# Rotary embedding of the queries: the cosine product stays in the PSUM bank, and the bank is freed one step later

## The reference, cut to what matters

```python
x = layernorm(x + gelu(einsum("bds,st->bdt", x, (w1 @ w2.T) * sparse_mask) + b2))  # applied per position of width 512
x = layernorm(x + cross_attention(x, ctx, ctx, mask, wq, wk, wv, wo))   # 32 query heads, 8 key heads
x = layernorm(x + x @ W.T + b + routed LoRA)
```

```python
x1, x2 = x[..., :64], x[..., 64:]
return concatenate([x1 * cos - x2 * sin, x2 * cos + x1 * sin], axis=-1)
```

## Time and profile before

| What | us |
|---|---|
| median of the three runs shown | 557.63 |
| the three runs | 554.43, 557.63, 2854.0 |
| the profiled execution: span from first to last instruction | 555.4 |
| TensorE busy | 510.5 (92%) |
| VectorE busy | 464.5 (84%) |
| ScalarE busy | 285.9 (51%) |
| GpSimd busy | 274.5 (49%) |
| one iteration of the loop (six alike, from 118 to 441.4) | 53.9 |

### The profile page before, as it was taken

The page is one execution under the profiler, slowest core; times in us unless marked ns, Lnnn a source line. Parts: engine busy times, 40 slices in busy tenths (PEclk is TensorE's granted clock), DMA queues, the critical chain, the costliest instruction groups (busy, mean ns, idle before and its releaser), DMA issues.

```text
span 555.4 us, 8155 instructions
## 1 busy us (share of the span) xinstructions
PE 510.5 (92%) x2637; PEld 419.9 (76%) x2637; DVE 464.5 (84%) x766; ACT 285.9 (51%) x494; POOL 274.5 (49%) x327
## 2 busy tenths in 40 slices
PE   5999788998999899989999999999899999979993
PEld 3776667886888687878877887788688788757882
DVE  3567877988899899989998899799979978989667
ACT  4373247763475347625761775267526642644423
POOL 2046445467256625652575267427723762316824
PEclk9999899999999999999999999999999999989998
DMA  8910220030103100320022011202020200300004
GB/s 301 342 39 1 73 80 1 1 113 6 71 2 113 40 36 0 113 75 0 23 90 76 0 56 57 76 0 96 17 76 0 76 1 8 52 1 0 2 1 151
DMA packets 27452, 31.45 MB, mean 57 GB/s; under 512 B 6177, under 2 KB 14625, under 8 KB 27434
## 3 DMA queue, kind: packets, MB, share of 16 engines
q1 hardware_dynamic: 27434, 31.22, 17.2%
HBM read 29.12 MB, written 2.10 MB: 56 GB/s over the span
## 4 chain that ended last, share of the span: by engine, by line
PE 54%; DVE 23%; issue 11%; ACT 5%; POOL 3%; DMA 2%; DVEq 0%; SPq 0%; ACTq 0%; POOLq 0%
PE bank L212 16%; PE bank L214 15%; PE bank L213 15%; PE bank L284 5%; DVE QR L951 5%; DVE VWl L850 3%; ACT QS L577 3%; PE bank L222 2%; DVE MX L968 2%; DVE PTl L850 2%; DVE QA L940 1%; ACT VWh L577 1%; DVE KR L935 1%; DMA WQr<-in_L_xattn_wq_dram 1%; DVE X L907 1%
## 5 line engine op out<-in xcount | busy, mean ns | idle before, releaser
L1393 POOL TENSOR_TENSOR PB<-SM,RI 128x512 f32<-128x512 f32 x32 | 34.1, 1067 | 149.1 <-DVE RI L981 149.1
L577 ACT ACTIVATE VWh<-bank 64x512 fp32r<-64x512 f32 x128 | 75.7, 591 | 61.1 <-PE bank L214 59.9
L577 ACT ACTIVATE QS<-bank 64x512 f32<-64x512 f32 x128 | 75.8, 592 | 59.1 <-DVE QR L951 49.3
L212 PE MATMUL bank<-XTh,WQh 128*128 128x512 f32 x256 | 101.3, 396 | 1.7 <-DVE XTl L850 1.7
L1381 POOL TENSOR_TENSOR QS<-QS,SIN 128x512 f32<-128x512 f32 x64 | 88.5, 1392 | 23.5 <-ACT QS L577 23.5
L213 PE MATMUL bank<-XTl,WQh 128*128 128x512 f32 x256 | 99.8, 390 | 0.0
L214 PE MATMUL bank<-XTh,WQl 128*128 128x512 f32 x256 | 99.8, 390 | 0.0
L850 DVE TENSOR_TENSOR VWl<-bank,VWh 64x512 fp32r<-64x512 f32 x128 | 88.1, 689 | 9.4 <-ACT VWh L577 6.4
L951 DVE TENSOR_TENSOR QR<-QA,QS 128x512 f32<-128x512 f32 x64 | 73.1, 1153 | 0.2
L284 PEld LDWEIGHTS bank<-KR,QR 128*128 128x128 f32 x512 | 61.0, 192 | 6.0 <-DVE QR L951 2.6
L284 PE MATMUL bank<-KR,QR 128*128 128x128 f32 x512 | 63.2, 276 | 1.5 <-DVE QR L951 1.5
(11 more groups left out here) (147 smaller groups left out, 973.5 us busy)
## 6 DMA issues: line engine op xcount, KB each, us to landing
WQr<-in_L_xattn_wq_dram SPq DMA_DIRECT2D x8, 1024.0 KB, 6.9
WOr<-in_L_xattn_wo_dram SPq DMA_DIRECT2D x8, 1024.0 KB, 5.3
KVr<-in_L_xattn_wk_dram SPq DMA_DIRECT2D x8, 256.0 KB, 2.7
KVr<-in_L_xattn_wv_dram SPq DMA_DIRECT2D x8, 256.0 KB, 3.7
out_dram<-X SPq DMA_DIRECT2D x8, 256.0 KB, 2.0
X<-in_x_dram SPq DMA_DIRECT2D x3, 512.0 KB, 10.1
WQr<-in_L_attn_w_dram SPq DMA_DIRECT2D x4, 256.0 KB, 3.8
WOr<-in_L_attn_w_dram SPq DMA_DIRECT2D x4, 256.0 KB, 5.7
```

What stands on the lines that cost most here:

```text
L212: pe.matmul(o, lh, rh, start=start, stop=False)
L577: return act.activation(o, i, ACT.Copy)
```

## The change

`q_cos` writes its product back to the bank that it reads, in place, and no longer to `QA`. `q_rot` reads that bank in place of `QA`. As the bank now holds the product until `q_rot` has read it, a query waits for `q_rot` of two queries back where it waited for `q_cos` of two queries back. Two waits of the weight transposes in the last group, which reuse the same banks, are changed in the same way. The lists of all engines keep their order, and no instruction is added or taken away. `QA` stays in use for other data in the first part of the kernel.

```diff
@@ def query(g, h, half) on TensorE
                 if counted(2 * G * g + 2 * h + half - 1):
-                    pe.wait_ge(sm["q_cos"], 2 * G * g + 2 * h + half - 1)
+                    pe.wait_ge(sm["q_rot"], 2 * G * g + 2 * h + half - 1)
@@ def weight_transpose(j) on TensorE
                 elif j < 3:
-                    pe.wait_ge(sm["q_cos"], 2 * G * HKV - 2 + j)
+                    pe.wait_ge(sm["q_rot"], 2 * G * HKV - 2 + j)
@@ def q_cos(g, h, half) on VectorE
                 dve.wait_ge(sm["q_swap"], i + 1)
-                dve.tensor_tensor(QA[:, half, :].rearrange("p (b s) -> p b s", b=2),
-                                  bank[:, Q_BANK + half, :].rearrange("p (b s) -> p b s", b=2),
-                                  by_pos(COS, 2, S), ALU.mult).then_inc(sm["q_cos"], 1)
+                q = bank[:, Q_BANK + half, :].rearrange("p (b s) -> p b s", b=2)
+                dve.tensor_tensor(q, q, by_pos(COS, 2, S), ALU.mult).then_inc(sm["q_cos"], 1)
@@ def q_rot(g, h, half) on VectorE
-                dve.tensor_tensor(QR[:, h % 2, half * HALF:(half + 1) * HALF], QA[:, half, :], QS[:, half, :],
+                dve.tensor_tensor(QR[:, h % 2, half * HALF:(half + 1) * HALF], bank[:, Q_BANK + half, :], QS[:, half, :],
                                   ALU.add).then_inc(sm["q_rot"], 1)
```

## The result

| | before | changed kernel |
|---|---|---|
| median of four runs, us | 556.86 | 678.63 (677.87 to 679.06) |
| ratio, with 95% interval | 1 | 1.221 [1.218, 1.224] |
| span of the profiled execution, us | 555.4 | 677.2 |
| mean granted clock over the span | 0.990 | 0.915 |
| one iteration of the loop, mean of six, us | 53.9 | 68.3 |

What follows compares the result with a forecast made beforehand. TensorE, busy 92% of the span, was taken as the bound. 555.4 us of span plus 80.3 of waits (6.6 + 58.8 + 14.9) and 6.0 for the clock gave 641.7, and 2.2 more for the median gave 644; range 624 to 666.

Steps and rivals of the forecast that it cites:

- The gain on VectorE: `q_rot` with one PSUM operand is as short as `q_cos`: 30 us less on VectorE, not on TensorE's path as such.
- `q_cos` to PSUM: On VectorE, `q_cos` writing its product to PSUM was taken as 0.69 us, between 682 ns and 1.28 us.
- Steps 1 to 6: One loop iteration, followed query by query through the waits for `q_rot`: 9.8 us longer, 58.8 over six iterations.
- step 6: Late in the iteration, queries (2,1) and (3,0) find their `q_rot` done; query(3,1) starts 0.4 us later.
- step 5: After query(2,0), 2.2 us are given back, 1.7 of them the waits before the attends for `pt_lo`.
- step 1: Start of the iteration: query(0,0) waits for `q_rot`(3,0) to end, a delay of 3.6 us.
- The clock term: TensorE's new pauses lower its clock, 1.7 us a fall at 14 places: 0 to 24 us, 6 taken.
- one in four: The share of the 14 pauses taken to lower TensorE's clock, giving 6 us.
- steps 1 and 4: The waits before queries (0,0) and (2,0), where matmuls pause some 4.5 us; the 14 places counted for the clock.
- `q_rot` stays contended: Rival: `q_rot` on VectorE is not shortened, 3.6 us in each of 7 groups, 25 more, 669 us; 5%.
- PSUM is slow: Rival: `q_cos` writing to PSUM takes 1.28 us, 0.6 more at four per group, 19 more, 663 us; 8%.

Runs made afterwards that it cites:

- e2_fill: The changed kernel with 302 extra matmuls, results unused, on TensorE ahead of the queries that wait for `q_rot`: 636.65 us, ratio 1.143.
- e3_rot01: The changed kernel with one VectorE instruction moved in the loop, `q_rot`(0,1) directly behind `q_rot`(0,0): 656.89 us, ratio 1.182.
- e1_wait_only: The kernel before with only the waits changed to `q_rot` of two queries back, data path still through `QA`: 720.38 us, ratio 1.294.
- second lists: VectorE, ScalarE and GpSimd lists rewritten again, one query moved on TensorE: 562.58 us with the change, 587.84 us on the data path of before.
- the third: The rewritten lists in a third version, with further instructions moved: 545.99 us with the change, 550.41 us on the data path and waits of before.
- the new lists: The third version of the rewritten lists, here on the data path and waits of the kernel before: 550.41 us, ratio 0.989.

## Why the prediction was wrong in its size

- **The gain on VectorE** (30 us from `q_rot`, off the path): right, 30.0 us. It did not make the kernel faster than before. VectorE's busy time fell by 40.6 in all; the other 10.6 were not foreseen.
- **`q_cos` to PSUM** (0.69 us taken, up to 1.28 in the range): 0.697.
- **Steps 1 to 6, the waits of an iteration**: right in place, order and size. Forecast 3.5, 2.3, 2.8 and 3 to 4 us before queries (0,0), (1,0), (1,1), (2,0), measured 3.42, 2.04, 2.61 and 2.89; step 6 had 0.4, measured 0.29; the waits for `pt_lo` are gone from the loop, as in step 5. With the clock held, `e2_fill` has 79.3 us more span than before, against 80.3. That the sum is so near is in part luck: by the starts of query(0,0), the six iterations are 55.4 us longer where the sum had 58.8, and from the last group's query(0,0) to the end it is 14.7 where it had 11.3 (the 14.9 less the 3.6 of step 1). The first group's 2.7, 2.7, 2.2 and 0.4 were 2.70, 2.70, 2.15 and 0.38.
- **The clock term**: the step that failed. It had 6.0 us, from "one in four" of 14 places and "steps 1 and 4" alone. Measured are 42.0, by `e2_fill` against the changed kernel. The price of one fall was right: 1.7 us forecast, and 42.0 us over the 24 falls that `e2_fill` took away is 1.75 each. Their number was wrong: 3.5 in the forecast, 14 at its upper end, 25 in the trace. The clock also fell after the shorter pauses, before queries (1,0) and (1,1), of 2.0 and 2.6 us, and kept up at the one before (2,0), of 2.9, which the term had counted as a place. The range ended at 666 because its upper end had 14 falls; with 42 in place of 6 the sum is 680. The iteration came out at 68.3 us for the 63 to 65 that the profile was to show.
- **Its premise.** "One in four" rests on the sentence that the pauses of 2.9 us before did not always lower the clock, and the trace of the kernel before says otherwise. It has two such pauses: 2.87 us before 491.38, with the fall of the earlier trace rows, and 2.96 us here, TensorE and the clock:

```profile
63.66 1.11 PE L222 MATMUL bank<-ID,X 128*128 128x128 f32 x4 [2.96 <-DVE X L907]
64.00:66.00 2.00, 2.00 (x11) 2.00 (x10) 2.00 (x3) 0.60 (x1) 0.73 (x1) 0.50 0.03 5
```

The clock was down behind both; behind the 2.10 us before 10.65 it stayed up. Every pause of the four in an iteration that is over 2 us was a place to count, at 1.7 us for each; 28 places would have been 48 us, nearer to the 42 than the 24 of the range's end.
- The Trainium skill (TensorE: Matmul & The Clock Gate, "HAM oscillation") describes a kernel in which each recurring pause lowers the clock anew. The trace agrees for 25 of 32 pauses, and not for each: 2.89 us before query(2,0) never did it in the loop of the changed kernel. In `e3_rot01` the same 2.89 us did, as its rows above show.
- The lower end of the range, 627, counts 9.0 us for the last group too, for which the steps had 14.9; with them it is 633. This did not matter, as the time lies above the range.
- **The rivals.** That `q_rot` stays contended and that PSUM is slow would have given 669 and 663, nearer to the time than the forecast, for reasons that the trace denies: `q_rot` never took over 693 ns, and `q_cos` 697 in the mean. A near number is not a cause. The first is what `e1_wait_only` does, and its price there was 41.8 us and not 25; the waits alone grew by 23.4, and the rest is again the clock, 0.87 against 0.915.
- The short `q_rot` held in all 64 of them, 637 to 693 ns, 38 of them beside a GpSimd instruction. By the rule of the Trainium skill (SBUF — State Buffer, "Who interferes with whom") an instruction of VectorE with a single SBUF input does not contend with GpSimd; the trace agrees.
- That this would make the change worthwhile did not follow, because the order of the lists decided whether the 0.47 us a `q_rot` counted at all: 41.8 us with the later wait and the old lists, 25.3 with the second lists, 4.4 with the third.

## What to carry to other kernels

When a buffer is handed back by a later step, write down for each user of the buffer where that step stands in its engine's list: what matters is not how much later the step is by itself (0.6 us here), but what stands between the two in the list (here, between q_cos(0,1) and `q_rot`(0,1), six other instructions, one of them a later query's own product). Move those steps first and make the change in the same edit. When TensorE will get recurring pauses, add the clock as a term for each pause and each repetition, with no fall and all falls as its ends. And compare a kernel with and without the change under the same lists, for lists that suit one data path are not the other's: here the new lists gave 5.9 us on the data path of before (556.31 to 550.41), and the change in them another 4.4.

## What the runs showed that I had not expected

- Matmuls whose result nobody reads made the kernel 42 us faster (678.6 to 636.7), by keeping the clock up.
- The clock fell after a pause of 2.04 us and kept up after 2.05, 2.70 and 2.89, in part with the same instructions ahead. What decides between them stays open; no run was made that varies only the length of one pause. A count of falls is thus a range, even where the pauses are known.
- A fall of the clock is paid inside the chain of waits: the query at half clock hands its bank on later, so the way from query(1,0) to query(1,1) took 7.2 us where 5.7 was worked out from durations at full clock.
- A product written in place in a PSUM bank costs VectorE 15 ns more than one into SBUF, 697 and 682 ns for 128x512 elements of 32 bits.
